# Two step-size products and the whole softplus in one step of a selective scan, with the positive part moved behind the third square

## The chip, the cores and the metric

The kernel runs on one core of one Trainium2 chip. The metric is the device time of one execution of the whole program, in microseconds (us). Times given as medians are medians of separate executions; the profile is of one further execution.

## The reference, cut to what matters

The program is a two-layer decoder over 32 sequences of 128 tokens with 128 channels. Eight stages run one after the other. The change touches one of them, the bidirectional selective scan, whose reference is, for each of two directions:

```
u       = silu(conv1d(x @ inW.T) + convB)            # 256 channels
dt,B,C  = split(u @ xpW.T)                           # 8, 16, 16 wide
delta   = softplus(dt @ dtW.T + dtB)
h_t     = exp(delta_t * A) * h_(t-1) + (delta_t * u_t) * B_t   # 16 states per channel
y_t     = sum_n h_t[n] * C_t[n]  ;  y = (y + u*D) * silu(z)
out     = y @ outW.T   ;   result = layernorm(x + 0.5*(forward + backward))
```

`softplus(v)` is computed as `relu(v) + log1p(exp(-|v|))`, and the logarithm by a polynomial of the eighth degree in `exp(-|v|)` that is factored into four quadratic factors, each a square plus a constant.

## The kernel before, in words

All 32 sequences lie in SBUF (`x_all`). The function `mamba` takes them in eight groups of four (`G = 4`). A group is worked in two halves, d=0 (forward) and d=1 (backward), and a half in sixteen steps s=0 to 15. A step is one pair of a chunk of two states (`C2 = 2`) and one of the two blocks of 128 channels (`DT = 2`), for all four sequences: 128 partitions by 1024 elements. The step's own work is spread over the engines:

- ScalarE (ACT): `exps`, line 2060, two exponentials that make the decay of the step; it is issued two steps ahead (`AHEAD = 2`), so at step s ACT makes the decay for step s+2.
- TensorE (PE): `b_rows`, line 1869, makes the input term in PSUM, one step ahead; `sum_states`, line 1888, sums the results of two steps into PSUM, at every odd step, for the states of two to three steps before, and waits for GpSimd's products (`hc_ready`).
- VectorE (DVE): the scan, line 2238, which needs the decay and the input term.
- GpSimd (POOL): the product of the scan's result with C, line 2166, in place; every second step also a diagonal matrix for PE, line 2142.
- SyncE (SP): the DMA that spreads C over the partitions.

Beside these steps each half prepares the other direction: while half d runs, everything that half 1-d needs is made, in steps named by constants. Silu of u and z (line 2028) is in step 3, B, C and dt (`bc_dt`, `b_columns`, lines 1829 and 1843, copied by ACT in lines 2031 and 2034) in step 5, the two products dt @ dtW (`delta_in`, line 1858) in steps 6 and 7, the softplus' scalar part (`softplus`, lines 2043 to 2052) with them, and its polynomial on DVE (`log1p`, line 2201, and `deltas`, line 2207) behind the scans of steps 8 to 12. GpSimd multiplies delta by u (line 2147) at step 13. Products for the groups to come are in steps 10, 12 (convolution) and 8, 13 (gate), and in d=0 there is the end of the group before: copied output (line 2010) in step 4, sum and moments (`total_of`, line 2219 and the norm's helpers) behind scan 6, the root on GpSimd (line 145) in step 7, `finish` (line 155, four instructions) behind scan 8. All orders are written out by hand: each engine runs its own list in program order, and waits on counted semaphores.

Within a step the order on ACT is: decay for step s+2, then the softplus part, then copies. On DVE it is: scan s, then the extra work of that step. On PE it is: `b_rows` for step s+1, then `delta_in` and other products, then `sum_states`.

In the kernel before ACT's part in step 6 is one biased copy of the first product out of PSUM (`pre`, line 2043); in step 7 the second biased copy, then absolute value (line 2046), exponential (line 2048), positive part (line 2049) and the four squares (line 2052). The wait behind the exponential (`steps.settle()`) stands behind the positive part, which does not need it. The small products pass through a ring of two PSUM banks (`ps_t`), with counts `filled` and `taken`; `fillings` tells how many are filled in a step, so that waits on those counts come out right.

There is one softplus ahead of the loop (in the prologue) and 15 in it: one in each of the eight halves d=0 and in each of the first seven halves d=1. Groups are counted from 0 below.

```
for s in range(S):
    ...
    exps(q + AHEAD, d if r < S else nd, r % S, ...)
    ...
    for t in range(DT):
        if s == AT_DELTA[t]:
            softplus(f, steps, nd, t, i * 2 + d + 1)
```

Of the kernel before, what the change touches and what calls it, by code (L numbers as in the profile page):

```python
# [8 lines left out]
ACT = mybir.ActivationFunctionType  # L9
# [1580 lines left out]
LOG1P_PAIRS = ((-2.3216868965700623, 0.43240693515853734), (-1.4247360163770746, 2.7021040781646755), (-0.08225193472242764, 3.257469309635712), (1.009357716033338, 1.1060625663063521))  # L1590
# [14 lines left out]
def mamba(nc, stage, x_all, c, p):  # L1605
# [3 lines left out]
    DT, N, R, W = 2, 16, D // 16, 4  # L1609
# [10 lines left out]
    with ExitStack() as stack:  # L1620
# [18 lines left out]
        pre = m.sb("pre", [128, DT, GT])  # L1639
# [69 lines left out]

        AT_X, AT_SILU, AT_BC, AT_DELTA, AT_LOG, AT_CONV, AT_Z = 1, 3, 5, (6, 7), (8, 9, 10, 11, 12), (10, 12), (8, 13)
        AT_DUT = (14, 15)
        AT_GATE, AT_OUT, AT_TOTAL, AT_ROOT, AT_FINISH = 2, 4, 6, 7, 8
        LAG = 3
# [1 line left out]
        def fillings(d, s, more):  # L1717


            head = d == 0 or more  # L1720
            n = (s == AT_OUT and d == 0)
            return n + head * (2 * (s == AT_BC) + (s in AT_DELTA) + (s in AT_DUT)) + more * ((s == AT_X and d == 0) + (s in AT_CONV) + (s in AT_Z))

        def fillings_before(d, s, more=True):

            return sum(fillings(0, r, more) for r in range(S if d else s)) + sum(fillings(1, r, more) for r in range(s if d else 0))
# [269 lines left out]
        def _(act):  # L1996
# [6 lines left out]
            def take(f, emit):  # L2003

                seq, bank = f.next()
                act.wait_ge(filled, seq + 1)
                emit(ps_t[:, bank, :]).then_inc(taken, 1)
# [31 lines left out]
            def softplus(f, steps, d, t, n):  # L2039

                if n is not None and t == 0:
                    act.wait_ge(delta_ready, n)
                take(f, lambda src: nc.scalar.activation(pre[:, t, :], src, ACT.Identity, bias=b_dt[:, d, t:t + 1]))
                if t == DT - 1:
                    act.wait_ge(taken, f.base + f.n + ALL_TAKEN)
                    steps.then(nc.scalar.activation(soft[:], pre[:], ACT.Abs))
                    steps.settle()
                    steps.then(nc.scalar.activation(soft[:], soft[:], ACT.Exp, scale=-1.0))
                    nc.scalar.activation(pre[:], pre[:], ACT.Relu)
                    steps.settle()  # L2050
                    for k in range(len(LOG1P_PAIRS)):
                        nc.scalar.activation(square[:, k, :, :], soft[:], ACT.Square, bias=centre[:, k:k + 1]).then_inc(square_ready, 1)

            def exps(q, d, s, spare=False):
# [8 lines left out]
            def group(i, more, first=False):  # L2063
                f = Fills(i * PER + PRO, PRO)
                steps = Steps(act, act_steps, i * 4 + 2, 4)
                for d in range(2):
                    head = d == 0 or more
                    nd = 1 - d
                    for s in range(S):
                        q = i * (2 * S) + d * S + s  # L2070
                        r = s + AHEAD
                        if r < S or head:
                            if r == S:
                                act.wait_ge(delta_ready, i * 2 + d + 2)
                            exps(q + AHEAD, d if r < S else nd, r % S, spare=first and d == 0 and r < SLOTS)
                        if s == AT_X and d == 0 and more:
                            copy_x(f)
                        if head:
                            if s == AT_SILU:
                                if not (first and d == 0):  # L2080
                                    act.wait_ge(g_ready, i * 2 + d)
                                silu(f, nd)
                            if s == AT_BC:
                                copy_bc(f, nd)
                                copy_b(f, nd)
# [3 lines that stand above are left out]
                                if s == AT_DUT[t]:  # L2089
                                    copy_du(f, nd, t)  # L2090
                        if more:
                            for t in range(DT):
                                if s == AT_CONV[t]:
                                    copy_u(f, d, t)
                                if s == AT_Z[t]:
                                    copy_z(f, d, t)
                        if s == AT_OUT and d == 0:
                            halve(f)
# [12 lines left out]
            for t in range(DT):  # L2111
                softplus(f, steps, 0, t, None)
# [856 lines left out]
def stage_mamba(nc, a, c):  # L2969
    mamba(nc, "mam", c.x_all, c, dict(a=a))  # L2970
# [83 lines left out]
```

## Time and profile before

| what | value |
| --- | --- |
| median of three runs | 2984.16 us |
| the three runs | 2984.16, 2980.74, 2984.37 us |
| the profiled execution's own time | 2980.29 us |
| span of its profile | 2978.5 us |
| busy share of PE, DVE, ACT, POOL over the span | 73%, 68%, 43%, 45% |
| mean granted TensorE clock over the span | 0.858 |

The span is the time from the first to the last recorded instruction, so 1.8 us of the profiled execution lie around it. The stage with the change runs from about 1537 us to 2460 us of the span, after a prologue that begins at about 1519 us. In the rows, a line such as "L2238 DVE" names the line of the kernel and the engine; a row of a timeline gives the start, how long the instruction (or a run of equal ones, x4) took, and in square brackets how long the engine sat idle before it and what ended that.

### The profile page before, as it was taken

To read this page: it belongs to the slowest core of one execution; us is meant where nothing else is said; L and a number is where in the kernel's file an instruction comes from. 1 tells how busy PE (TensorE), PEld (TensorE's weight loads), DVE (VectorE), ACT (ScalarE), POOL (GpSimd) and SP (SyncE) were. 2 spreads that over 40 slices of the span, in tenths; PEclk is the share of its full clock that TensorE was granted. 3 is DMA by queue.
4 is the path that set the end of the run, shared out by engine and by line. 5 is a ranking of instruction groups with operands and counts; after the bars stand their busy time and mean duration, and the time that the engine had idled before them with its cause. 6 is when DMAs were issued, how large, how long until landed. Compare 5 with 4: busy or idle time off the path is not lost. (4 is left out here: it accounts for less than half of the span.)

```text
span 2978.5 us, 48740 instructions
## 1 busy us (share of the span) xinstructions
PE 2170.8 (73%) x19339; PEld 1332.8 (45%) x19339; DVE 2018.7 (68%) x3250; ACT 1295.4 (43%) x1935; POOL 1328.2 (45%) x1015
## 2 busy tenths in 40 slices
PE   3888656764476699899679899999999875552704
PEld 1455445543255455555434554555555443431303
DVE  5564446886454355555438888978988876888598
ACT  1444325553255422222156667566666632220460
POOL 3432244555332000000038898898898883232001
PEclk8899778897687899999889999999999997665856
DMA  3331010000333100000022222222222211000001
GB/s 103 88 80 38 9 35 17 17 16 4 97 93 76 51 1 1 1 1 1 20 65 76 72 88 71 72 83 83 65 83 75 70 57 32 22 8 8 0 0 29
DMA packets 135553, 134.57 MB, mean 45 GB/s; under 512 B 22544, under 2 KB 128801, under 8 KB 132129
## 3 DMA queue, kind: packets, MB, share of 16 engines
q1 hardware_dynamic: 127776, 129.89, 15.4%
q8 instruction: 155, 2.54, 0.4%
q10 hardware_dynamic: 7552, 1.58, 0.3%
q14 instruction: 70, 0.57, 0.1%
HBM read 109.14 MB, written 15.99 MB: 42 GB/s over the span
## 5 line engine op out<-in xcount | busy, mean ns | idle before, releaser
L2166 POOL TENSOR_TENSOR mam_h<-mam_h,mam_c_all 128x1024 f32<-128x1024 f32 x256 | 657.4, 2582 | 89.0 <-DVE mam_h L2238 88.9
L2238 DVE TENSOR_TENSOR_SCAN mam_h<-mam_decay,mam_ps_b 128x1024 f32<-128x1024 f32 x256 | 574.4, 2274 | 99.0 <-PE mam_ps_b L1869 96.7
L1869 PEld LDWEIGHTS mam_ps_b<-mam_diag,mam_duT 64*128 64x128 f32 x4096 | 251.7, 190 | 219.3 <-DVE mam_h L2238 135.9
L2060 ACT ACTIVATE mam_decay<-mam_delta,mam_a_neg 128x508 f32<-128x508 f32 x512 | 331.4, 710 | 32.8 <-DVE mam_h L2238 28.5
L1869 PE MATMUL mam_ps_b<-mam_diag,mam_duT 64*128 64x128 f32 x4096 | 297.4, 287 | 56.0 <-DVE mam_h L2238 44.3
L745 DVE TENSOR_REDUCE at_top<-at_ps_s 128x8 f32<-128x1024 f32 x128 | 156.7, 1224 | 203.7 <-PE at_ps_s L470 202.8
L1888 PE MATMUL mam_ps_y<-mam_h,all_ident 64*64 64x512 f32 x2048 | 253.7, 611 | 13.8 <-POOL mam_h L2166 13.8
L1461 ACT ACTIVATE moe_silu<-moe_ps_g 128x512 f32<-128x512 f32 x144 | 86.0, 597 | 286.0 <-PE moe_ps_g L1408 259.3
L1411 PE MATMUL moe_ps_u<-moe_ynT,moe_w_up 128*128 128x512 f32 x288 | 157.3, 629 | 34.8 <-DVE moe_hidden L1544 34.8
L609 ACT ACTIVATE at_e<-at_ps_e 128x1024 f32<-128x1024 f32 x128 | 131.0, 1023 | 117.5 <-PE at_ps_e L470 113.5
L1544 DVE TENSOR_TENSOR moe_hidden<-moe_silu,moe_ps_u 128x512 f32<-128x512 f32 x144 | 96.9, 686 | 95.3 <-PE moe_ps_u L1411 90.7
L2142 POOL TENSOR_TENSOR mam_diag<-mam_halves,mam_b_col 128x512 f32<-128x512 f32 x128 | 137.0, 1070 | 41.8 <-ACT mam_b_col L2034 41.8
L1408 PE MATMUL moe_ps_g<-moe_ynT,moe_w_gate 128*128 128x512 f32 x288 | 154.8, 620 | 0.8 <-ACT moe_ynT L1453 0.8
L1421 PEld LDWEIGHTS moe_ps_d<-moe_w_down,moe_hidden 128*128 128x128 f32 x1152 | 140.2, 193 | 33.1 <-issue 33.1
L2504 POOL TENSOR_TENSOR xat_e<-xat_e,xat_inv 128x2048 f32<-128x2048 f32 x16 | 72.0, 4502 | 171.9 <-DVE xat_inv L2526 171.9
L1421 PE MATMUL moe_ps_d<-moe_w_down,moe_hidden 128*128 128x128 f32 x1152 | 139.7, 276 | 0.0
L1817 PE MATMUL mam_ps_t<-mam_xT,mam_w_tap 128*128 128x512 f32 x256 | 134.3, 653 | 1.5 <-ACT mam_xT L2017 1.5
L1888 PEld LDWEIGHTS mam_ps_y<-mam_h,all_ident 64*64 64x64 f32 x2048 | 69.5, 133 | 145.8 <-issue 144.9
L145 POOL TENSOR_TENSOR moe_after_rstd<-moe_after_var,all_minus_half 128x4 f32<-128x4 f32 x8 | 8.1, 1008 | 244.5 <-DVE moe_after_var L140 244.5
L2665 PE MATMUL qua_ps_x<-qua_w_T,qua_hidden 128*128 128x128 f32 x192 | 30.2, 335 | 113.9 <-DVE qua_hidden L2739 113.9
L1555 DVE SCALAR_TENSOR_TENSOR moe_acc<-moe_ps_d,moe_combine,moe_acc 128x128 f32<-128x128 f32 x256 | 72.0, 344 | 56.8 <-PE moe_ps_d L1421 56.8
L1200 POOL TENSOR_TENSOR ret_head_rstd<-ret_head_var,ret_minus_half 128x16 f32<-128x16 f32 x32 | 92.8, 2900 | 36.7 <-DVE ret_head_var L1230 36.7
(350 smaller groups left out, 4445.1 us busy)
## 6 DMA issues: line engine op xcount, KB each, us to landing
mam_c_all<-mam_c_rows SPq DMA_DIRECT2D x256, 256.0 KB, 3.5
at_rows<-at_split SPq DMA_DIRECT2D x64, 192.0 KB, 2.9
at_q<-at_rows SPq DMA_DIRECT2D x32, 192.0 KB
at_k<-at_rows SPq DMA_DIRECT2D x32, 192.0 KB
at_q<-at_rows SPq DMA_DIRECT2D x32, 128.0 KB
at_k<-at_rows SPq DMA_DIRECT2D x32, 128.0 KB
all_x_all<-in_x SPq DMA_DIRECT2D x8, 256.0 KB, 4.8
at_q<-at_rows SPq DMA_DIRECT2D x32, 64.0 KB
```

What stands on the lines that cost most here:

```text
L609: nc.scalar.activation(e[:, b % 2, 2 * x:2 * x + 2, :, :].rearrange("p k j t -> p (k j t)"), ps_e[:].rearrange("p r j t -> p (r j t)"), AC ...
L745: nc.vector.tensor_reduce(top[:, b % 2, :, NJ * x:NJ * x + NJ], ps_s[:], AX_X, ALU.max).then_inc(top_ready, 1)
L1408: nc.tensor.matmul(ps_g[:, k, :], w_gate[:, e, k * 128:(k + 1) * 128], ynT[:], start=True, stop=True).then_inc(gate_ready, 1)
L1411: last = nc.tensor.matmul(ps_u[:, k, :], w_up[:, e, k * 128:(k + 1) * 128], ynT[:], start=True, stop=True)
L1421: last = nc.tensor.matmul(ps_d[:, o % 2, b, :], hidden[:, o % 2, k, b * T:(b + 1) * T], w_down[:, e, k, :], start=(k == 0 and b == 0), sto ...
L1817: last = nc.tensor.matmul(ps_t[:, bank, :], w_tap[:, d, k, t * 128:(t + 1) * 128], xT[:, d, :, k:k + T], start=(k == 0), stop=(k == W - 1))
L1869: last = nc.tensor.matmul(ps_b[:, slot, odd, :, at // 2, x:x + HT], duT[r, d, s % DT, at, :], diag[r, chunk % SLOTS, at, :, :], start=True ...
L1888: last = nc.tensor.matmul(ps_y[t * HT:(t + 1) * HT, r, :], c.ident[rows, rows], h[rows, (s + t) % H_SLOTS, :, n, :, :].rearrange("p o g t ...
L2060: last = nc.scalar.activation(decay[:, s % SLOTS, :, n, :, 1:T], src, ACT.Exp, scale=a_neg[:, d, s % DT, st:st + 1])
L2142: nc.gpsimd.tensor_tensor(diag[:, set_chunk % SLOTS, :, :, :], one, column, ALU.mult).then_inc(diag_ready, 1)
L2166: nc.gpsimd.tensor_tensor(flat(h[:, slot, :, :, :, :]), flat(h[:, slot, :, :, :, :]), flat(c_all[:, chunk, :, :, :, :]), ALU.mult).then_in ...
L2238: nc.vector.tensor_tensor_scan(row(h[:, s % H_SLOTS, :, :, :, :]), row(decay[:, s % SLOTS, :, :, :, :]), row(ps_b[:, s % 2, :, :, :, :]), ...
```

## The change

Both products dt @ dtW are made in step 6 and both biased copies and the whole scalar part of the softplus run in step 6 on ACT. So step 7 holds nothing of it. The number of fillings in that step is counted accordingly. In the softplus, the positive part moves from before the wait on the exponential to between the third and the fourth square.

```
-        AT_X, AT_SILU, AT_BC, AT_DELTA, AT_LOG, AT_CONV, AT_Z = 1, 3, 5, (6, 7), (8, 9, 10, 11, 12), (10, 12), (8, 13)
+        AT_X, AT_SILU, AT_BC, AT_DELTA, AT_LOG, AT_CONV, AT_Z = 1, 3, 5, (6, 6), (8, 9, 10, 11, 12), (10, 12), (8, 13)
...
-            return n + head * (2 * (s == AT_BC) + (s in AT_DELTA) + (s in AT_DUT)) + more * (...)
+            return n + head * (2 * (s == AT_BC) + DT * (s == AT_DELTA[0]) + (s in AT_DUT)) + more * (...)
...
                     steps.then(nc.scalar.activation(soft[:], pre[:], ACT.Abs))
                     steps.settle()
                     steps.then(nc.scalar.activation(soft[:], soft[:], ACT.Exp, scale=-1.0))
-                    nc.scalar.activation(pre[:], pre[:], ACT.Relu)
                     steps.settle()
                     for k in range(len(LOG1P_PAIRS)):
+                        if k == len(LOG1P_PAIRS) - 1:
+                            nc.scalar.activation(pre[:], pre[:], ACT.Relu)
                         nc.scalar.activation(square[:, k, :, :], soft[:], ACT.Square, bias=centre[:, k:k + 1]).then_inc(square_ready, 1)
```

## Rows read from the trace of the kernel before

**Rows 1.** The page's costliest groups: busy us, mean ns, idle before and its releaser.
```profile
L2166 POOL TENSOR_TENSOR mam_h<-mam_h,mam_c_all 128x1024 f32<-128x1024 f32 x256 | 657.4, 2582 | 89.0 <-DVE mam_h L2238 88.9
```
**Rows 2.** Busy time by stretch, group 0's d=1 to group 1's: PE, PEld, DVE, ACT, POOL, clock.
```profile
1620.00:1735.50 115.50, 105.40 (x1008) 58.34 (x1008) 100.19 (x58) 76.03 (x108) 104.18 (x52) 1.00 0.26 77
```
**Rows 3.** Waits in the stage, 1540 to 2450 us: total us, times, longest.
```profile
POOL mam_h L2166 <- DVE mam_h L2238: 88.9, 39, 5.4
...
DVE mam_poly L2201 <- ACT all_y_all L2052: 35.9, 15, 3.6
```
**Rows 4.** Timeline of POOL in group 0, d=1: products of steps 8 and 9.
```profile
1620.22 2.35 POOL L2166 TENSOR_TENSOR mam_h<-mam_h,mam_c_all 128x1024 f32<-128x1024 f32 x1
1626.06 3.25 POOL L2166 TENSOR_TENSOR mam_h<-mam_h,mam_c_all 128x1024 f32<-128x1024 f32 x1 [3.48 <-DVE mam_h L2238]
```
**Rows 5.** Timeline of DVE in group 0, d=1: scans 7 and 8, polynomial, scan 9.
```profile
1612.67 4.46 DVE L2238 TENSOR_TENSOR_SCAN mam_h<-mam_decay,mam_ps_b 128x1024 f32<-128x1024 f32 x2 [2.61 <-PE mam_ps_b L1869]
1620.74 2.91 DVE L2201 SCALAR_TENSOR_TENSOR mam_poly<-all_y_all,mam_soft 128x1024 f32<-128x1024 f32 x1 [3.60 <-ACT all_y_all L2052]
1623.69 2.29 DVE L2238 TENSOR_TENSOR_SCAN mam_h<-mam_decay,mam_ps_b 128x1024 f32<-128x1024 f32 x1
```
**Rows 6.** Timeline of ACT in group 0, d=1: the softplus, and the decay for step 9.
```profile
1613.78 0.69 ACT L2043 ACTIVATE mam_pre<-mam_ps_t,mam_b_dt 128x512 f32<-128x512 f32 x1 [2.62 <-PE mam_ps_t L1858]
1614.36 1.31 ACT L2060 ACTIVATE mam_decay<-mam_delta,mam_a_neg 128x508 f32<-128x508 f32 x2
1615.86 0.69 ACT L2043 ACTIVATE mam_pre<-mam_ps_t,mam_b_dt 128x512 f32<-128x512 f32 x1 [0.18 <-PE mam_ps_t L1858]
1616.58 1.06 ACT L2046 ACTIVATE mam_soft<-mam_pre 128x1024 f32<-128x1024 f32 x1
1617.67 1.06 ACT L2048 ACTIVATE mam_soft<-mam_soft 128x1024 f32<-128x1024 f32 x1
1618.63 1.04 ACT L2049 ACTIVATE mam_pre<-mam_pre 128x1024 f32<-128x1024 f32 x1
1619.58 4.25 ACT L2052 ACTIVATE all_y_all<-mam_soft,mam_centre 128x1024 f32<-128x1024 f32 x4
```
**Rows 7.** Timeline of ACT in the prologue: the two biased copies back to back.
```profile
1520.17 0.69 ACT L2043 ACTIVATE mam_pre<-mam_ps_t,mam_b_dt 128x512 f32<-128x512 f32 x1 [1.21 <-PE mam_ps_t L1858]
1521.03 0.69 ACT L2043 ACTIVATE mam_pre<-mam_ps_t,mam_b_dt 128x512 f32<-128x512 f32 x1 [0.17 <-PE mam_ps_t L1858]
```
**Rows 8.** Timeline of PE in group 0, d=1: the input term for step 8.
```profile
1613.61 1.16 PE L1869 MATMUL mam_ps_b<-mam_diag,mam_duT 64*128 64x128 f32 x16
```
**Rows 9.** Timelines of ACT and DVE in group 2, d=1: first copy, scan 9.
```profile
1846.17 0.69 ACT L2043 ACTIVATE mam_pre<-mam_ps_t,mam_b_dt 128x512 f32<-128x512 f32 x1 [2.63 <-PE mam_ps_t L1858]
...
1854.53 2.29 DVE L2238 TENSOR_TENSOR_SCAN mam_h<-mam_decay,mam_ps_b 128x1024 f32<-128x1024 f32 x1
```
**Rows 10.** Timeline of DVE in group 1, d=0: sum, polynomial, finish.
```profile
1667.53 4.89 DVE L2219 TENSOR_TENSOR mam_total<-mam_half,all_x_all 128x512 f32<-128x512 f32 x1
...
1679.09 1.23 DVE L2201 SCALAR_TENSOR_TENSOR mam_poly<-all_y_all,mam_soft 128x1024 f32<-128x1024 f32 x1 [0.64 <-ACT all_y_all L2052]
1680.35 3.80 DVE L155 TENSOR_SCALAR all_x_all<-mam_total,mam_after_moments,mam_after_rstd 128x128 f32<-128x128 f32 x4
```
**Rows 11.** Timeline of POOL in group 1, d=0: products 6 to 8 and the root.
```profile
1669.50 2.36 POOL L2166 TENSOR_TENSOR mam_h<-mam_h,mam_c_all 128x1024 f32<-128x1024 f32 x1
1676.35 2.36 POOL L2166 TENSOR_TENSOR mam_h<-mam_h,mam_c_all 128x1024 f32<-128x1024 f32 x1 [4.49 <-DVE mam_h L2238]
1678.67 1.01 POOL L145 TENSOR_TENSOR mam_after_rstd<-mam_after_var,all_minus_half 128x4 f32<-128x4 f32 x1
1679.65 1.57 POOL L2142 TENSOR_TENSOR mam_diag<-mam_halves,mam_b_col 128x512 f32<-128x512 f32 x1
1681.19 2.37 POOL L2166 TENSOR_TENSOR mam_h<-mam_h,mam_c_all 128x1024 f32<-128x1024 f32 x1
```
**Rows 12.** Timeline of DVE in the prologue: the polynomial's parts 2 to 4.
```profile
1528.45 3.74 DVE L2201 SCALAR_TENSOR_TENSOR mam_poly<-all_y_all,mam_poly 128x1024 f32<-128x1024 f32 x3
```

More of the change, by code:

```diff
@@ L1708, in mamba @@
         ALL_TAKEN = 2
-        AT_X, AT_SILU, AT_BC, AT_DELTA, AT_LOG, AT_CONV, AT_Z = 1, 3, 5, (6, 7), (8, 9, 10, 11, 12), (10, 12), (8, 13)
+        AT_X, AT_SILU, AT_BC, AT_DELTA, AT_LOG, AT_CONV, AT_Z = 1, 3, 5, (6, 6), (8, 9, 10, 11, 12), (10, 12), (8, 13)
         AT_DUT = (14, 15)
@@ L1721, in fillings @@
             n = (s == AT_OUT and d == 0)
-            return n + head * (2 * (s == AT_BC) + (s in AT_DELTA) + (s in AT_DUT)) + more * ((s == AT_X and d == 0) + (s in AT_CONV) + (s in AT_Z))
+            return n + head * (2 * (s == AT_BC) + DT * (s == AT_DELTA[0]) + (s in AT_DUT)) + more * ((s == AT_X and d == 0) + (s in AT_CONV) + (s in AT_Z))
         def fillings_before(d, s, more=True):
@@ L2048, in softplus @@
                     steps.then(nc.scalar.activation(soft[:], soft[:], ACT.Exp, scale=-1.0))
-                    nc.scalar.activation(pre[:], pre[:], ACT.Relu)
                     steps.settle()
                     for k in range(len(LOG1P_PAIRS)):
+                        if k == len(LOG1P_PAIRS) - 1:
+                            nc.scalar.activation(pre[:], pre[:], ACT.Relu)
                         nc.scalar.activation(square[:, k, :, :], soft[:], ACT.Square, bias=centre[:, k:k + 1]).then_inc(square_ready, 1)
```

## The prediction

> **What bounds the kernel now.** I read the page's costliest groups first, then the busy time by stretch, then the waits of the stage, and last the timelines of four engines around one softplus. The largest group is GpSimd's product: 256 of it take 657 us of the stage's 920, and GpSimd idles 89.0 us before them, nearly all released by a scan [rows 1]. In one turn of the loop, 115.5 us, GpSimd is busy 104.2, DVE 100.2 and ACT 76.0 [rows 2]. So the time of a turn is GpSimd's work plus the holes in it, and a microsecond more or less in such a hole is a microsecond of the program, as long as GpSimd has no other hole behind it to take it up; it has none, for its next products run one on another until the next half's softplus. The waits tell who makes the holes: 89.0 us over 39 waits for scans, and the polynomial on DVE waits 35.9 us over 15 for ACT's squares [rows 3], once in each softplus of the loop.
>
> One such hole, group 0, d=1: GpSimd ends product 8 at 1622.57 and begins product 9 at 1626.06 [rows 4], because scan 9 started only at 1623.69. In front of scan 9 DVE idled 3.60 us for the first square and then took 2.91 for one polynomial part [rows 5], where 1.23 is its length when nothing is in its way [rows 10]. It ended 1.08 behind GpSimd's product 8: both read SBUF, and the later one waited for the earlier.
>
> **The change on ACT.** I count from the start of the first biased copy, T (1613.78 in [rows 6]), which the change leaves where it is: TensorE makes the first product in step 6 as before. Before: decay for step 9 at T+0.58, second copy at T+2.08, absolute value +2.80, exponential +3.89, positive part +4.85, squares +5.80 to +10.05. First square usable by DVE at 1620.74, T+6.96 [rows 5, 6].
>
> After: the second product follows the first at once on PE. Back to back, the copies start 0.86 apart [rows 7]. Absolute value 0.72 later, exponential 1.09 after that [rows 6], T+2.67. The first square no longer has the positive part ahead of it, but stands behind the wait; I price that wait by the same 1.09 that the absolute value shows before the exponential. First square T+3.76, usable 1.16 later at T+4.92: **2.04 us earlier than before**. Squares follow each other at 1.03 ((4.25 - 1.16) / 3): three of them reach to T+6.85, where the positive part starts; its follower starts 0.95 behind it, so the fourth square at T+7.80, and the next instruction at T+8.84.
>
> What is moved behind all that is the decay for step 9, which stood ahead of the softplus and now stands in step 7 behind it: T+8.84, 1.31 long [rows 6], done at T+10.15. The scan of step 9 needs it. **So scan 9 can't start before T+10.20.** What was early on ACT (T+0.58 to 1.89, eight us before scan 9) becomes the last thing that scan 9 waits for. The positive part itself costs ACT the same 1.04 in either place; deltas read it only at step 12.
>
> **What that does in each of the 15 halves.**
> - Five like rows 5 (group 0, 1, 4, 5, 6, d=1): scan 9 started at T+9.91 to 9.93 [rows 5, 6]. Now T+10.20: +0.28 each, +1.4.
> - Three where the polynomial's first part had little or no product in its way: T+8.36 in [rows 9], and 8.61 and 8.22 in group 3, d=1, and group 0, d=0. Now T+10.20: +1.84, +1.59, +1.98, together +5.4. The gain in the first square is worth nothing to them.
> - One (group 4, d=0) at T+10.19: nothing.
> - Six (groups 1, 2, 3, 5, 6, 7, d=0), where sum, moments and finish keep DVE: scan 9 at T+12.1 hides the late decay. Here DVE waited 0.64 for the first square (five times, 0.29 once) [rows 10]; now the first part can start when scan 8 ends, at 1678.45. Product 7 on GpSimd ends at 1678.71, the root follows, then diagonal, product 8 [rows 11]. Finish takes 3.80 instead of some 1.1 because its parts stand behind the diagonal and product 8, and ends 0.6 after product 8 (1683.56). So what counts is when product 8 ends. The diagonal was held by the polynomial, 1.57 against 1.04. If the part slips in at 1678.8, behind the root's short read, it ends near 1680.0 in place of 1680.32, diagonal and product 8 come 0.3 earlier, and scan 9 too: -0.3. Bounds: -0.64 (all of the wait); above, the sum in [rows 10]: it came during a product and took 4.89 us, until after diagonal and product 6 (1671.86). If the part is kept out like that until product 8 ends (some 1683.0), finish ends at 1685.2: +1.06. I take -0.3, since the root was not lengthened by a polynomial part that overlapped it (1.01 in rows 11), so its hold is short. Five times -0.3 and once 0: -1.5.
>
> **The rest.** PE: the second product now stands ahead of the input term for step 8 [rows 8], which comes about 1.05 later; scan 8 ends at T+4.3 instead of +3.35 [rows 5], before the first square is usable and before product 8 needs it at 1620.22 [rows 4]. Hidden; if it weren't, 1 us a half. `sum_states` behind both keeps its place, and the ring of two banks has both free, as ACT copied B and C out before. SP and GpSimd's lists and the DMAs aren't moved. Port holds: the polynomial's first part may now collide with product 7 or the diagonal in the uncovered halves and push product 8 by up to 1.1; GpSimd has a hole of 3.48 behind it [rows 4]. The prologue has nothing to hide ACT: there DVE's four parts end at 1532.19 [rows 12]. The first square comes 0.9 earlier, the fourth 0.1 later, so the last part starts at the fourth square's end and the stage begins **0.5 earlier**.
>
> **Sum:** +1.4 + 5.4 + 0 - 1.5 - 0.5 = +4.8 us. Against the profiled execution, 2978.5 of span and 1.8 around it, 2985.1. The median of the three runs is 3.9 above that execution; carried to it, 2984.16 + 4.8 = 2989.0. About 0.2%, 6 us, is what a measurement of this kernel can tell from no change (the three runs alone lie 3.6 apart), so this sits inside it, near the upper edge.
>
> **Rivals.**
> 1. *The root stands behind the polynomial* in the six covered halves. The part comes 0.22 before product 7 ends; if it takes the read path at that moment, the root waits until 1679.8 and ends near 1680.6, as a product that starts just behind a part is lengthened by 0.9 (3.25 against 2.35) [rows 4]. Finish waits for the root, the diagonal too: +0.3 instead of -0.3, total +8.1, 2992.3. For it: GpSimd's next instruction did wait in all such cases of long instructions. Against: the sum of [rows 10] was passed over by a diagonal and a product.
> The Trainium skill (SBUF — State Buffer, practical consequences) has the pair of ports as an exclusive lock, which whoever issues first holds for the whole instruction. By that rule the part would go in at product 7's end and the root behind it, this rival's 2992.3; rows 10 with its 4.89 doesn't fit "first come" as simply.
> 2. *Slower clearly:* the part is kept out until product 8 ends, as the sum was. Place: the same six halves. Price +1.06 each, 6.4: total 6.8 - 0.5 + 6.4 = +12.7, 2996.9. It decides if GpSimd's list, ready one behind another, leaves no gap at 1678.71.
> 3. *Faster:* the late decay isn't what scan 9 waits for, and the earlier square lets the part go in ahead of product 8, ending at T+6.5 instead of T+9.9: up to 3.4 in five halves and 2 in three, some -20, 2964. That needs the decay for step 9 done by T+6.6. ACT's order in the code forbids it, as four squares (4.1) alone reach past that. A gain elsewhere: the sum in d=0 fell right in one of seven (1.0 instead of 4.89; that turn was 1.9 shorter); if the shifts make it fall right always, -11. Nothing in the rows speaks for it, since the steps between are paced by GpSimd and shift with it.
> 4. *No change:* what is lost at scan 9 is taken up later, as when TensorE is late for another reason; 2984.
>
> **How the numbers follow.** Forecast 0.50; root behind 0.20; kept out 0.13; faster 0.09 (both kinds); taken up 0.08. Of the forecast's half, 0.35 falls within 0.2% and 0.15 above, as its bounds are +3 (all of 0.64 gained) to +6.3 (nothing gained in the covered halves), another 1.5 if the copies start 1.05 apart, as the input term and the product take on PE [rows 8], and a median moves by 2 to 3. Root behind gives 0.05 within and 0.15 above, kept out 0.13 above, taken up 0.08 within. So faster 0.09, same 0.48, slower 0.43. The range goes from 2980 (a low run of the forecast case) to 2997 (rival 2), and leaves out the faster cases and the top of rival 2.
>
> **What would show it.** On ACT a group of two copies 0.86 apart, then all of the softplus, then a run of four or more decays. On DVE the wait of the polynomial for squares falls from 35.9 to about 8 x 0.7 us, while scan 9 now waits for the decay of line 2060, a row that hardly exists before, and starts at T+10.2 in nine halves. GpSimd's hole before product 9 is 0.3 to 2 longer there. The turn of [rows 2] takes about the same, 115.5 us, as one half gains the 0.3 that the other loses. I am wrong if scan 9 starts before T+10 in an uncovered half, if the covered halves change by more than 0.7, or if input term 8 shows up as a releaser of scan 8 that moves product 8.

## The result, and the profile after

| | before | after |
|---|---|---|
| median of 9 runs | 2984.16 (2980.74 to 2988.57) | 2990.96 (2986.47 to 2998.44) |
| ratio to before | | 1.0028 [1.0017, 1.0039] |
| profiled execution, its span | 2980.29, 2978.5 | 2991.73, 2989.9 |
| mean granted clock | 0.858 | 0.850 |
| loop: first biased copy in it to last scan's start | 880.9 | 885.7 |

Slower by 6.8 us in the medians; a second comparison (e9, below) gave 1.0014 [1.0005, 1.0023]. So by the two ratios the change costs 0.14 to 0.28%, 4 to 8 us. 2989.0 was forecast.

The two profiled executions lie 11.4 apart, and not all of it is the change's. The stage begins 3.9 later (first biased copy of the prologue at 1524.06 against 1520.17), though no edit acts ahead of it. The prologue is 0.4 shorter. The loop takes 4.8 more. From the last scan to the last finish it is 19.9 against 17.4, and 0.6 more comes behind the stage. The end of the stage goes with the granted clock:

The windows view of after: a stretch in the loop and one at the stage's end; columns as in [rows 2].
```profile
1650.00:1660.00 10.00, 9.32 (x102) 6.84 (x102) 5.66 (x3) 5.12 (x9) 10.00 (x6) 0.83 0.27 77
2449.00:2470.00 21.00, 10.95 (x76) 7.29 (x73) 5.99 (x14) 0.60 (x1) 7.69 (x4) 0.84 0.00 0
```
The column behind POOL is the mean granted clock of the stretch. Before shows 0.99 from 2440 to 2460, and its last 32 matmuls of line 1902 took 3.84 where after's took 5.83. The 0.83 of the first row comes back below.

**The change does what it says.** T is, as in the prediction, the start of the first biased copy of a half. "The part" below is the polynomial's first part on DVE, "the port" the access to SBUF that the part and GpSimd's instructions keep each other from, as the waits in these rows show. A half d=0 is "covered" where the sum took 4.88 and sum, moments and finish of the group before so keep DVE busy over the softplus; the other halves are "uncovered". The softplus of group 0, d=1, on ACT, to be held against [rows 6]; T is 1619.31:
```profile
1619.31 1.49 ACT L2043 ACTIVATE mam_pre<-mam_ps_t,mam_b_dt 128x512 f32<-128x512 f32 x2 [2.63 <-PE mam_ps_t L1858]
1620.83 1.06 ACT L2046 ACTIVATE mam_soft<-mam_pre 128x1024 f32<-128x1024 f32 x1
1621.91 1.06 ACT L2048 ACTIVATE mam_soft<-mam_soft 128x1024 f32<-128x1024 f32 x1
1623.01 3.23 ACT L2053 ACTIVATE all_y_all<-mam_soft,mam_centre 128x1024 f32<-128x1024 f32 x3
1626.14 1.04 ACT L2052 ACTIVATE mam_pre<-mam_pre 128x1024 f32<-128x1024 f32 x1
1627.09 1.13 ACT L2053 ACTIVATE all_y_all<-mam_soft,mam_centre 128x1024 f32<-128x1024 f32 x1
1628.13 2.53 ACT L2061 ACTIVATE mam_decay<-mam_delta,mam_a_neg 128x508 f32<-128x508 f32 x4
```
Two copies back to back, four squares from T+3.70 (3.76 predicted), the positive part behind the third, and only then the decay for step 9, at T+8.82 (8.84). DVE over the same time, against [rows 5]:
```profile
1618.21 2.29 DVE L2239 TENSOR_TENSOR_SCAN mam_h<-mam_decay,mam_ps_b 128x1024 f32<-128x1024 f32 x1 [2.61 <-PE mam_ps_b L1869]
1621.21 2.29 DVE L2239 TENSOR_TENSOR_SCAN mam_h<-mam_decay,mam_ps_b 128x1024 f32<-128x1024 f32 x1 [0.71 <-PE mam_ps_b L1869]
1624.19 5.04 DVE L2202 SCALAR_TENSOR_TENSOR mam_poly<-all_y_all,mam_soft 128x1024 f32<-128x1024 f32 x1 [0.69 <-ACT all_y_all L2053]
1629.64 2.29 DVE L2239 TENSOR_TENSOR_SCAN mam_h<-mam_decay,mam_ps_b 128x1024 f32<-128x1024 f32 x1 [0.41 <-ACT mam_decay L2061]
```
Scan 8 starts 0.71 behind scan 7 and ends at T+4.19, hidden as forecast. The polynomial's first part starts at T+4.88 (4.92 predicted), 2.08 earlier than before. It then takes 5.04 where 1.23 is its own length: the whole gain in the squares lies in that one row. And scan 9 waits for the decay, until T+10.33. GpSimd, against [rows 4]:
```profile
1620.11 4.70 POOL L2167 TENSOR_TENSOR mam_h<-mam_h,mam_c_all 128x1024 f32<-128x1024 f32 x2
1624.76 1.06 POOL L2143 TENSOR_TENSOR mam_diag<-mam_halves,mam_b_col 128x512 f32<-128x512 f32 x1
1625.76 2.38 POOL L2167 TENSOR_TENSOR mam_h<-mam_h,mam_c_all 128x1024 f32<-128x1024 f32 x1
1632.00 3.24 POOL L2167 TENSOR_TENSOR mam_h<-mam_h,mam_c_all 128x1024 f32<-128x1024 f32 x1 [3.86 <-DVE mam_h L2239]
```
The part came 0.62 before product 7 ended, but diagonal and product 8 ran ahead of it (to 1628.14), each at its own length; 1.1 behind product 8 it ended. The hole before product 9 is 3.86 instead of 3.48.

In the waits of the stage, to be held against [rows 3] (us, times, longest):
```profile
POOL mam_h L2167 <- DVE mam_h L2239: 88.8, 39, 5.7
...
DVE mam_h L2239 <- ACT mam_decay L2061: 9.9, 13, 2.7
DVE mam_poly L2202 <- ACT all_y_all L2053: 7.9, 12, 0.7
```
The polynomial's wait fell from 35.9 to 7.9, and GpSimd's for scans stayed as it was. The row of the decay is new but for 0.3 us, once, before.

That GpSimd's total stayed hides two changes. The holes before product 9 grew from 50.7 to 56.5 us over the 15 halves, and those before product 7, where scan 7 stands behind sum and moments, fell from 30.2 to 24.2, since more sums were short (below). GpSimd idled 83.5 us in the loop before and 83.4 after. The loop's 4.8 lies in GpSimd's own instructions, 797.4 us before and 802.3 after: among them product 8 took 3.2 more over all halves, the root 3.0 and product 6 1.1. The holes ahead of product 7 are of the halves d=0.

Three of the halves in which finish covers the softplus are left. Group 3, d=0 (T=1909.50), DVE and then GpSimd, against [rows 10, 11]:
```profile
1915.73 1.43 DVE L2202 SCALAR_TENSOR_TENSOR mam_poly<-all_y_all,mam_soft 128x1024 f32<-128x1024 f32 x1
1918.14 3.83 DVE L155 TENSOR_SCALAR all_x_all<-mam_total,mam_after_moments,mam_after_rstd 128x128 f32<-128x128 f32 x4 [0.98 <-POOL mam_after_rstd L145]
1922.00 2.29 DVE L2239 TENSOR_TENSOR_SCAN mam_h<-mam_decay,mam_ps_b 128x1024 f32<-128x1024 f32 x1
```
```profile
1913.72 2.37 POOL L2167 TENSOR_TENSOR mam_h<-mam_h,mam_c_all 128x1024 f32<-128x1024 f32 x1 [4.49 <-DVE mam_h L2239]
1916.04 2.00 POOL L145 TENSOR_TENSOR mam_after_rstd<-mam_after_var,all_minus_half 128x4 f32<-128x4 f32 x1
1918.00 1.05 POOL L2143 TENSOR_TENSOR mam_diag<-mam_halves,mam_b_col 128x512 f32<-128x512 f32 x1
```
Here the part came 0.36 before product 7's end and did go in at it (1.43). The root, 1/256 of a product in size, started behind it and took 2.00 instead of 1.01; finish waited 0.98 for it, and scan 9 starts at T+12.50 instead of T+12.06. That is rival 1.

**The loop, half by half**, as worked out from the starts of the first biased copies (us from one to the next; the last entry is to the last scan). The first half, group 0's d=0, took 53.25 before and 55.33 after.

| group | before: d=1 to d=0, to d=1 | after |
|---|---|---|
| 0 | 58.34, 57.07 | 60.37, 55.36 |
| 1 | 58.36, 58.62 | 60.33, 55.36 |
| 2 | 56.81, 58.42 | 58.77, 57.53 |
| 3 | 58.66, 55.21 | 60.33, 55.35 |
| 4 | 58.37, 57.08 | 58.77, 57.53 |
| 5 | 58.35, 57.06 | 58.77, 55.34 |
| 6 | 58.37, 76.97 | 58.79, 77.78 |

A turn with nothing special in it took 115.45 before (group 4) and 116.30 after: +0.41 in the half behind an uncovered scan 9, +0.45 behind a covered one. Two patterns differ. 55.3 is a half with a short sum just ahead of its T (1.00 to 1.57 instead of 4.88): moments and finish then no longer cover the softplus, scan 9 comes at T+10.33 instead of 12.50, and the half is 2.2 shorter. 60.3 is a half with a stretch of lower clock (0.83 above, so part of it at the lower of the clock's two levels, 1.2 instead of 2.4 GHz; line 1869's group of 16 took 2.05 there instead of 1.16), 1.6 longer, and each time the sum at its end was short. Before has one short sum (group 3 to 4), after has four. A further profile of after (e9) has 60.3 in the same three places and once more, so the pattern comes back from one execution to the other. Over the 84 stretches of 10 us from 1570 to 2410 the clock is below full at 7 places in before and at 13 and 14 in the two profiles of after. In e4, e10 and e11 below, whose scan 9 is early, it is at 6 or 7. That the longer stop ahead of scan 9, in which TensorE has less to do, brings these on would fit, but e2 below speaks against it: it has 13 such places, and its scan 9 comes at T+9.95 at the latest in the halves d=1. What brings them on stays open.

### The profile page after: what moved, and what is told of

Read it like the earlier page. It is cut to its first block and busy times, and to the rows that moved or that the text cites. A ratio compares the mean times of both kernels' runs of the same rounds, so it can differ in the third digit from the quotient of the medians.

```text
span 2989.9 us, 48740 instructions
## 1 busy us (share of the span) xinstructions
PE 2187.4 (73%) x19339; PEld 1346.5 (45%) x19339; DVE 2031.8 (68%) x3250; ACT 1297.0 (43%) x1935; POOL 1334.0 (45%) x1015
## 5 line engine op out<-in xcount | busy, mean ns | idle before, releaser
L2167 POOL TENSOR_TENSOR mam_h<-mam_h,mam_c_all 128x1024 f32<-128x1024 f32 x256 | 662.3, 2603 | 88.8 <-DVE mam_h L2239 88.8
```

Source lines behind the costliest of these rows:

```text
L2167: nc.gpsimd.tensor_tensor(flat(h[:, slot, :, :, :, :]), flat(h[:, slot, :, :, :, :]), flat(c_all[:, chunk, :, :, :, :]), ALU.mult).then_in ...
```

## The experiments

My theory: in an uncovered half scan 9 is held by the late decay (T+10.3), in a covered one by the root. The rival: it is held by the port, since the part is kept out until product 8 has ended (T+9.95), and the decay hardly matters. In the profile of after the two lie 0.4 apart, so both had to be taken away singly and together. All kernels compute the full reference. Each ratio is to runs of the kernel before on the same chip; the chips of e1 to e4, of e5 to e8 and of e9 to e11 differ, so between these sets ratios are compared and not times. "Loop" is of one profiled execution.

| run | what it is | ratio to before | loop |
|---|---|---|---|
| e1 | after, decay for step 9 early | 1.0009 [0.9997, 1.0020] | 884.4 |
| e2 | before, positive part moved | 1.0011 [0.9998, 1.0024] | 884.3 |
| e3 | after, positive part back | 1.0043 [1.0027, 1.0060] | 890.9 |
| e4 | e1, root first, GpSimd gives way | 0.9898 [0.9878, 0.9919] | 850.0 |
| e5 | e4 with the decay late | 1.0040 [1.0027, 1.0053] | 891.6 |
| e6 | before, root first, gives way | 0.9998 [0.9989, 1.0007] | 880.3 |
| e7 | after, root first | 1.0019 [1.0007, 1.0032] | 887.5 |
| e8 | e1 and root first | 0.9992 [0.9982, 1.0002] | 877.2 |
| e9 | after once more | 1.0014 [1.0005, 1.0023] | 888.0 |
| e10 | e8, gives way in step 8 alone | 0.9894 [0.9879, 0.9909] | 847.5 |
| e11 | e4 without the sum's wait | 0.9923 [0.9910, 0.9937] | 862.5 |

**e1: the decay alone.**
```
-    if r < S or head:
+    if (r < S or head) and not (head and s == AT_DELTA[0] + 1):
         ...
+    if head and s == AT_DELTA[0]:
+        exps(q + AHEAD + 1, d, r + 1)
```


> The changed kernel, with the decay for step 9 issued ahead of the softplus in step 6, in ACT's idle time before the first biased copy. Theory A (scan 9 waits for the late decay): scan 9 no longer waits for line 2060's decay in any half. Where DVE's first polynomial part is kept out until product 8 ends, scan 9 moves from T+10.33 only to T+9.95 (0.4 in each of seven halves), in group 0, d=0 to about T+8.1 (2.2), in the halves where the sum was short to about T+9.8 (0.5 each): some 5 to 7 us under the changed kernel, 2984 to 2986, near the kernel before. Theory B (the loss is all GpSimd and DVE keeping each other off SBUF, the late decay is hidden behind it): scan 9 starts where it did and the time stays at 2991.


Measured: scan 9 never waits for a decay. Group 1, d=1 (T=1729.12), on DVE:
```profile
1734.00 4.05 DVE L2204 SCALAR_TENSOR_TENSOR mam_poly<-all_y_all,mam_soft 128x1024 f32<-128x1024 f32 x1 [0.69 <-ACT all_y_all L2053]
1738.08 2.29 DVE L2241 TENSOR_TENSOR_SCAN mam_h<-mam_decay,mam_ps_b 128x1024 f32<-128x1024 f32 x1
```
It starts at T+8.07 in the first half and at T+8.7 to 9.9 in the others uncovered, but the part still takes 3.8 to 5.0 in d=1, and covered halves stay at T+12.5. The time is that of before or a little above. It is 0.05 to 0.2% below after's two ratios, but the intervals overlap: the time alone doesn't show the gain, the offsets do. So both are true: the decay held scan 9, and the port keeps most of what the decay lets go.

**e2 and e3: the parts of the change singly.** e2 is before with the positive part moved behind the third square; e3 is after with it put back ahead of the first.


> The kernel before with only the positive part moved behind the third square; both products and the softplus stay in steps 6 and 7. Theory A: the decay for step 9 keeps its place ahead, so scan 9 doesn't wait for it; first square 0.85 earlier (T+6.1), which gains 0.85 in the three halves where nothing was in its way and 0.5 in the prologue, nothing in the five where the part ends behind product 8 anyway, and costs 0.4 in the six covered halves if the part there comes in before the root and holds it up: within 2 us of 2984. Theory C (the moved positive part is what delays ACT): the loss of the change stands here too, 2990.

> The changed kernel with the positive part put back ahead of the squares; products and softplus in step 6. Theory A: scan 9 waits for the decay of step 9 as in the changed kernel (T+10.2, the positive part costs ACT the same in either place), the prologue's 0.5 is given back: 2990 to 2992. The first square at T+5.7 instead of T+4.9 makes no difference in the loop. Theory C: the loss is gone, 2984.


In e2 the first square comes at T+6.16. Scan 9 starts at T+9.90 to 9.95 in six halves d=1, at 8.06 and 9.54 in group 0's two, and at T+12.52 to 12.54 in five covered ones. So the 0.85 expected in three halves did not come: their 8.22, 8.36 and 8.61 became 8.06, 9.90 and 9.94. On GpSimd in group 3, d=0:
```profile
1906.82 2.37 POOL L2167 TENSOR_TENSOR mam_h<-mam_h,mam_c_all 128x1024 f32<-128x1024 f32 x1 [4.48 <-DVE mam_h L2239]
1909.13 2.00 POOL L145 TENSOR_TENSOR mam_after_rstd<-mam_after_var,all_minus_half 128x4 f32<-128x4 f32 x1
```
Either part alone brings the root's cost: in e3 too the root takes 1.99 and scan 9 starts at T+12.51 in covered halves, as its first square comes at T+5.68, ahead of scan 8's end there (T+6.32). In e3 scan 9 waits for its decay in all d=1 halves, at T+10.19. Neither part gains by itself, and of the three e3 loses most: its loop is 10 longer than before's, and 1.0043 is above the 2990 to 2992 expected. It had one short sum and after four, which would account for it; no run isolates that.

**e4: everything taken away.** To e1 the root ahead of product 7 is added, and waits by which GpSimd lets DVE's waiting instruction in (the sum in step 6, part 1 in step 8, finish, parts 2 and 4, the delta).
```
     ...
+    if s == AT_TOTAL and d == 0 and not first:
+        pool.wait_ge(total_ready, i)
+    if s == AT_LOG[0] and head:
+        pool.wait_ge(dve_steps, part_done)
+    if s == AT_FINISH and d == 0 and not first:
+        pool.wait_ge(x_ready, i * G)
     ...
+    if s == AT_ROOT and d == 0 and not first:
+        after.root(nc, pool, c, i - 1)
     pool.wait_ge(h_ready, q + 1)
+    if head and s - AT_LOG[0] in (1, 3):
+        pool.wait_ge(dve_steps, part_done + s - AT_LOG[0])
+    if head and s == AT_LOG[-1]:
+        pool.wait_ge(delta_ready, i * 2 + d + 2)
     ...
-    if s == AT_ROOT and d == 0 and not first:
-        after.root(nc, pool, c, i - 1)
     ...
```


> The changed kernel, with the decay for step 9 first, GpSimd's root ahead of its product 7, and GpSimd made to wait, at five places of a half, until DVE's polynomial part (steps 8, 9, 11, delta at 12), the sum (step 6, d=0) or the finish (step 8, d=0) is done. Theory A with the port as read from the traces (a DVE instruction with two inputs in SBUF that comes while GpSimd runs one long product behind another is kept out until GpSimd pauses, and costs 3 to 4 us for its 1.1): GpSimd loses 1.1 at each place and gets product 9 at about T+10.0 instead of T+12.3 to 14.4; some 1.5 to 2 us less in each of 15 halves, 2955 to 2965. Rival D: waits on GpSimd only move its idle time, as each semaphore wait and the later parts take back what the first gives; 2980 to 2995, or slower.


Measured, in group 0, d=1 (T=1621.06) on DVE:
```profile
1625.94 1.23 DVE L2216 SCALAR_TENSOR_TENSOR mam_poly<-all_y_all,mam_soft 128x1024 f32<-128x1024 f32 x1 [0.69 <-ACT all_y_all L2053]
1627.20 2.29 DVE L2253 TENSOR_TENSOR_SCAN mam_h<-mam_decay,mam_ps_b 128x1024 f32<-128x1024 f32 x1
```
The part takes 1.2 to 1.7, scan 9 starts at T+6.1 to 7.4, the loop is 31 shorter and the program 1.0% faster, 33 us of the medians where I had expected 19 to 29. The early square is worth that much once nothing eats it, as e6 confirms.

**e5 and e6: is each condition needed?** e5 is e4 with the decay for step 9 back behind the softplus; e6 is before (late squares, early decay) with e4's waits and root.


> e4_give_way with the decay for step 9 back behind the softplus, as in the changed kernel; root ahead of product 7 and GpSimd giving way at the five places stay. Theory A: scan 9 waits for the decay in all 15 halves, at T+10.2 to 10.3, where in e4 it started at T+6.1 to 7.4; GpSimd gets product 9 at about T+13.8 instead of T+10.8, some 3 us in each half: 40 to 45 us over e4, 2985 to 2997. Rival (the decay's place is worth no more than the 7 us that e1 gained): 2956 to 2960.

> The kernel before, with only the root ahead of product 7 and GpSimd giving way at the five places; products in steps 6 and 7, positive part ahead of the squares, decay for step 9 ahead of the softplus by its place. First square at T+6.96 instead of T+4.88 in e4, so GpSimd waits longer in step 8; scan 9 at about T+8.2, product 9 at about T+12.7. If the change's early squares are worth something once GpSimd gives way: 1.5 to 2 us a half more than e4, 2972 to 2980. If giving way is all and the early squares are nothing: 2949 to 2953.


e5, group 0, d=1 (T=1616.49), DVE:
```profile
1621.37 1.23 DVE L2214 SCALAR_TENSOR_TENSOR mam_poly<-all_y_all,mam_soft 128x1024 f32<-128x1024 f32 x1 [0.69 <-ACT all_y_all L2053]
...
1626.82 2.29 DVE L2251 TENSOR_TENSOR_SCAN mam_h<-mam_decay,mam_ps_b 128x1024 f32<-128x1024 f32 x1 [4.22 <-ACT mam_decay L2061]
```
The part is free, and scan 9 stands until T+10.33 in every half, 3.0 to 4.2 us behind it. That is the late decay's full price, 42 us (1.0040 less 0.9898, of 2984); in after all but 0.4 of it lies under the time that the port takes anyway. e6 is as fast as before: giving way gains nothing while the square is late. Three conditions, then (early square, early decay, free port), and the change meets one. The root's new place is in e4, e5 and e6 alike and was not left out singly; by e8 below it gains nothing without the waits.

**e7 and e8: the root.** Both move the root ahead of product 7 (diff in e4), in after and in e1.


> The changed kernel with GpSimd's root issued ahead of product 7 instead of behind it, no other edit. Behind product 7 now stands the diagonal and product 8 at once. Theory A with 'kept out while products follow one on another': the first polynomial part of a covered half, which took 1.43 in the changed kernel and stretched the root to 2.0, now takes about 4.9 and ends 1.1 behind product 8; finish runs in 1.1 at once behind it, scan 9 at about T+12.2 instead of T+12.5. Near no change against the changed kernel: 2988 to 2991. By a lock that is given in order of arrival the part would still take 1.4, the root would be out of the way, scan 9 would start at T+10.3 (the decay) to 11.6, and the kernel would be 4 to 10 us faster than the changed one.

> e4_give_way without the giving way: the changed kernel with the decay for step 9 first and the root ahead of product 7. If the waits on GpSimd are what e4 gained by: 2980 to 2986, like e1. If the two reorderings brought it: 2949 to 2955.


e7, group 1, d=0 (T=1682.00), GpSimd:
```profile
1684.00 1.01 POOL L145 TENSOR_TENSOR mam_after_rstd<-mam_after_var,all_minus_half 128x4 f32<-128x4 f32 x1 [2.26 <-DVE mam_after_var L140]
...
1688.55 2.03 POOL L2143 TENSOR_TENSOR mam_diag<-mam_halves,mam_b_col 128x512 f32<-128x512 f32 x1
```
The root has its 1.01 again, the part (1.43) goes in ahead of the diagonal, which takes 2.03, and scan 9 comes at T+11.54 instead of 12.50. I had expected the part to be kept out for 4.9 and scan 9 at T+12.2: a miss, taken up in the last section. What came was the other outcome on record, the lock given in order of arrival, in its offset and not in its 4 to 10 us. The time didn't improve by what the offset did. Of e7's 12 runs five lie near 2980.6 and seven at 2987 to 2994, with its profile from the upper end, so e7 tells little. With the decay early as well (e8) the time is before's, 0.08% less at an interval that holds none.

**e10 and e11: which waits count?** e10 is e8 with the waits for part 1 and for finish alone; e11 is e4 without the sum's.


> e8_decay_root (decay for step 9 first, root ahead of product 7) with GpSimd giving way in step 8 alone: to the first polynomial part, and in d=0 to finish. If each place pays for itself: product 9 starts some 2 us earlier in all halves, and 15 to 25 us of e4's gain stand here. If a polynomial part that comes long before the end of a product with the next one ready is passed over: the second part, behind scan 9, comes 1.2 us before the end of product 8 with product 9 ready, is kept out until after it, and gives the gain back; within 5 us of e8, 2973 to 2980.

> e4_give_way without the wait for the sum in step 6 of d=0; the four other places stay. The sum goes back to 4.9 us in the seven halves that have one and scan 7 starts later. If what DVE loses there reaches GpSimd: the hole before product 7 grows by 1 to 3 us, 7 to 15 us over e4, 2956 to 2964. If product 9's place behind finish takes it up: 2949 to 2953.


Of the two outcomes on record for e10, giving the gain back at part 2 did not come, and the other (15 to 25 us of e4's gain) was put too low: against e8 it is 29 us faster by the ratios. Its ratio is the lowest of all, with an interval that overlaps e4's. Group 0, d=1 (T=1620.41), DVE and GpSimd:
```profile
1625.29 1.23 DVE L2210 SCALAR_TENSOR_TENSOR mam_poly<-all_y_all,mam_soft 128x1024 f32<-128x1024 f32 x1 [0.69 <-ACT all_y_all L2053]
1626.55 2.29 DVE L2247 TENSOR_TENSOR_SCAN mam_h<-mam_decay,mam_ps_b 128x1024 f32<-128x1024 f32 x1
1628.75 2.30 DVE L2210 SCALAR_TENSOR_TENSOR mam_poly<-all_y_all,mam_poly 128x1024 f32<-128x1024 f32 x1
```
```profile
1620.14 4.70 POOL L2176 TENSOR_TENSOR mam_h<-mam_h,mam_c_all 128x1024 f32<-128x1024 f32 x2
1626.59 1.05 POOL L2145 TENSOR_TENSOR mam_diag<-mam_halves,mam_b_col 128x512 f32<-128x512 f32 x1 [1.75 <-DVE mam_poly L2210]
1627.60 5.68 POOL L2176 TENSOR_TENSOR mam_h<-mam_h,mam_c_all 128x1024 f32<-128x1024 f32 x2
```
GpSimd waits 1.75 ahead of the diagonal instead of 3.86 behind product 8. Part 2 comes during product 8 but gets in at its end (1629.97), ahead of product 9, whose scan ended only when part 2 started. Over the program, in e10's costliest groups:
```profile
L2176 POOL TENSOR_TENSOR mam_h<-mam_h,mam_c_all 128x1024 f32<-128x1024 f32 x256 | 658.5, 2589 | 17.1 <-DVE mam_h L2247 17.1
```
17.1 is what is left of the 88.8 us of holes ahead of products. Part of the difference now stands elsewhere: in the loop GpSimd waits 12.4 us for the part, 18.6 for finish and 6.8 ahead of the root, and idles 49.4 in all instead of 83.5, which is the loop's gain of 33. In e11 the sum took 4.88 in all seven places, scan 9 of d=0 came at T+8.85, and the loop was 12.5 longer than e4's: that is what the sum's wait is worth there. In e10 the sum was short in four of seven without it.

**e9: after once more**, beside e10 and e11.


> The changed kernel itself once more, beside the two below and the kernel before on one chip, because 7 us are to be told from the scatter of single runs: 1.0015 to 1.004 of the kernel before.


1.0014 is just below the range expected. Its loop took 888.0, 2.3 more than the first profile's, with the same offsets: 10.33 in the uncovered halves.

## Why the prediction was right, and where it wasn't

- **Scan 9 not before T+10.20:** right in kind and 0.13 low. T+10.32 to 10.34 in twelve of fifteen halves, since a scan starts 0.2 behind its decay where I took 0.05. The first term, +0.28 for each of five halves, was +0.41.
- **The three halves at +1.84, +1.59, +1.98:** only the last stands (53.25 to 55.33). The other two are the step of mine that failed: I took T for fixed and read 8.36 and 8.61 as time gained. Before, T itself stood late there, with 58.62 and 58.42 for a half of 57.1, so the early scan 9 only caught up, and the change could take no more from them than from the rest. That was rival 4's mechanism, in two halves.
- **Covered halves, -0.3:** false, and rival 1, to which I gave 0.20, is what happened, at +0.44 instead of its +0.3 in two halves and +0.80 in the last: the root takes the part's time on top of its own. In the other three the sum was now short, and scan 9 came 1.7 earlier. A change of more than 0.7 was on my list of what would show me wrong, and on the covered halves I was. The Trainium skill (SBUF — State Buffer, Who interferes with whom, practical consequences) has whoever issues first hold the shared pair of ports for the whole instruction and the other wait; the root's 2.00 and e7's diagonal of 2.03 agree, as the sum of [rows 10] doesn't.
- **The sum in step 6:** of rival 3 I said that nothing speaks for more short sums. There were four in place of one, each worth 2.2, in three cases with 1.6 lost just before in a stretch of lower clock. What makes a sum short stays open.
- **The sum +4.8** met the loop's +4.8 by luck of the signs (and it held -0.5 for the prologue, so for the loop itself it said +5.3). Its true terms: first half +2.1; six turns at +0.86 and the last half with its end +1.2, 8.5 together; and less 3.7 for the short sums net of the lower clock. Nor did it come as holes, in which I had reckoned it: they stayed at 83.5 in the loop, and the 4.8 lies in longer instructions on GpSimd. That GpSimd has no other hole to take a gain or loss up was a wrong reading too: 30.2 of the 88.9 us lie ahead of product 7. Rival 2 (kept out in the covered halves) did not come, but the same keeping-out took the part in the uncovered ones, where I had noted it as a collision with room behind it. There it was free only because the decay was late too.
- **Prologue -0.5:** -0.44. **Input term hidden:** yes. **Polynomial's wait 5.6:** 7.9. **Turn 115.5 as before:** 116.3, since the covered half loses too.

So the change makes one of three things early. The square comes 2.1 earlier; the part that reads it is passed over by GpSimd until T+9.9; and the decay that the same edit put behind it comes at T+10.1. e1 takes away the last and gets 0.05 to 0.2% back, within the noise; with the root as well (e8) only the port is left, and the time is before's; e4 and e10 take away all.

## What to carry to other kernels

When an instruction on a path is made earlier, ask for each thing that its successor needs, and for the port it goes through, when it comes; and look at what the edit itself moved behind. A queue that is always released ahead can keep its neighbour out for several instructions: one wait of the engine that bounds the kernel, at the place where the other is about to ask, is a hole of 1.75 here in place of one of 3.86, and of 2.7 where GpSimd waits for finish as well. Before a small offset is read as a gain, look whether its origin stood late.

## What the runs showed of the hardware that I had not expected

**A waiting DVE instruction can be passed over twice.** I took DVE's polynomial parts, deltas and sums (each reads two tiles from SBUF) that became ready during a product on GpSimd, in the profiles of before, after and e1 to e8. Where GpSimd's next instruction followed without a gap and DVE's came 0.59 us or more before the product's recorded end, 57 of 61 were passed over by GpSimd's next two instructions and took 4.9 to 5.1 us, for an instruction of 1.0 to 1.2; the other four, all sums, took 1.6. Where it came 0.55 or less before the end, 124 of 125 got in at the end. Where GpSimd paused behind the product, all 130 got in. Both kinds can be seen above: 5.04 with 0.62 to go, 1.43 with 0.36. e7's part came 0.36 before the end, which fits my 4.9 for it having failed.

The time to the end is not the whole rule. Where the instruction came during a diagonal, 17 first parts (in e1, e2, e3 and e7) with 0.25 to 0.84 to go were passed over by the product behind it, 11 others with 0.45 to 0.88 got in at its end, and so did all 210 with 0.96 or more. And in e10, which is not in the count, part 2 came 0.8 to 1.3 before product 8's end and got in in all 15 halves; there product 9 was released only when part 2 was. That GpSimd's next instruction stands ahead where it was released earlier is my reading; it fits e10, but no run was made to try it.

**A small instruction pays in full.** The root (128x4) took 1.01 alone and 2.00 behind a part of 1.43; it ended 0.88 behind the part.
